# Edge pass of a graph attention layer: the group's transpositions on PE moved ahead of the encoding, their readers moved forward on DVE and ACT, the factor one step later

## The reference

```
h = (x @ W.T).reshape(n, H, D)                       # 6250 nodes, 8 heads of 32
alpha = sum(h[src] * a_src) + sum(h[dst] * a_dst)    # 200000 edges, sorted by dst
enc = relu(edge_attr @ edge_W.T + edge_b)
alpha = leaky(alpha + sum(enc * h[dst]))             # slope 0.2
amax = segment_max(alpha, dst)
ex = exp(alpha - amax[dst])
denom = segment_sum(ex, dst)
out = segment_sum(h[src] * ex / denom[dst], dst)
```

## Time and profile before

| | us |
| --- | --- |
| median of 3 runs | 5372.19 |
| lowest, highest | 5364.89, 5379.21 |
| profiled execution, own time | 5386.62 |
| its span, first to last instruction | 5384.8 |
| PE, DVE, ACT, POOL busy | 3894.4, 2587.7, 2125.3, 2060.0 |

### The profile page before, as it was taken

One profiled execution on the slowest core, in us unless ns is written; L12 is line 12 of the kernel. 1 busy time (PEld: TensorE's weight loads), 2 busy tenths in 40 slices (PEclk: granted clock), 3 DMA queues, 4 the chain that ended last, 5 costly groups with the idle time before them and its releaser, 6 DMA issues.

```text
span 5384.8 us, 88907 instructions
## 1 busy us (share of the span) xinstructions
PE 3894.4 (72%) x22054; PEld 2499.9 (46%) x22055; DVE 2587.7 (48%) x6056; ACT 2125.3 (39%) x5703; POOL 2060.0 (38%) x2172
## 2 busy tenths in 40 slices
PE   4778995676776666777676676666667767791999
PEld 3357884343343333333333333333333334580888
DVE  6556553554554455555454554454455546341121
ACT  3212331444444444444444444444444445342322
POOL 4120003454554454454444444444445443005111
PEclk8889998787787788788887887888788878895999
DMA  4610112333333333333333333333333332201110
GB/s 153 213 37 22 35 33 70 83 93 90 92 95 90 91 100 90 92 96 95 93 93 93 91 93 92 97 92 93 95 92 102 96 93 72 103 27 53 34 35 30
DMA packets 352302, 449.27 MB, mean 83 GB/s; under 512 B 170970, under 2 KB 275163, under 8 KB 350456
## 3 DMA queue, kind: packets, MB, share of 16 engines
q0 software_dynamic: 95568, 267.78, 19.0%
q10 hardware_dynamic: 108050, 122.83, 7.4%
q1 hardware_dynamic: 148231, 53.53, 4.1%
HBM read 389.57 MB, written 55.13 MB: 83 GB/s over the span
## 4 chain that ended last, share of the span: by engine, by line
PE 38%; another core or an unknown queue 21%; issue 11%; DVE 9%; ACT 9%; ACTq 7%; DMA 3%; DVEq 2%; POOL 1%; SPq 0%; POOLq 0%
ACT dist L770 5%; PE bank L1040 5%; PE bank L1183 4%; PE bank L1195 4%; PE bank L1061 3%; PE bank L1143 3%; PE bank L1005 3%; PE bank L1014 3%; ACTq L737 3%; PE bank L1099 3%; PE bank L1030 2%; ACTq L735 2%; DVEq L355 2%; DVE msg L1540 1%
## 5 line engine op out<-in xcount | busy, mean ns | idle before, releaser
L514 POOL DMA_INDIRECT al<-h_tab,idx x976 | 1022.8, 1048 | 1110.0 <-issue 1104.5
L752 ACT ACTIVATE enc<-bank,eb 128x512 f32<-128x512 f32 x880 | 556.3, 683 | 1768.5 <-remote 1213.1
L514 POOL DMA_INDIRECT gbuf<-h_tab,idx x784 | 793.4, 1012 | 906.4 <-issue 877.4
L1061 PE MATMUL bank<-prod,hsel 128*32 128x128 f32 x7040 | 351.1, 328 | 1001.4 <-DVE carry L1505 444.8
L1040 PE MATMUL bank<-oneh_t,hbt 125*128 125x512 bf16 x2640 | 865.1, 478 | 6.9 <-issue 3.5
L1061 PEld LDWEIGHTS bank<-prod,hsel 128*32 128x32 f32 x7040 | 200.3, 126 | 1190.2 <-DVE carry L1505 474.9
L1099 PE MATMUL bank<-msg,oneh 128*125 128x264 f32 x2352 | 648.2, 422 | 64.9 <-DVE r L1549 47.2
L1460 DVE SCALAR_TENSOR_TENSOR prod<-enc,adst,bank 128x512 f32<-128x512 f32 x880 | 629.4, 737 | 21.4 <-PE bank L1040 7.1
L770 ACT ACTIVATE dist<-iota_n,dtile 128x125 f32<-128x125 f32 x1760 | 550.8, 384 | 0.5
L1099 PEld LDWEIGHTS bank<-msg,oneh 128*125 128x125 f32 x2352 | 468.0, 207 | 173.1 <-issue 87.2
L1549 DVE TENSOR_TENSOR r<-r,bank 125x264 f32 x440 | 188.1, 428 | 614.7 <-issue 282.4
(11 more groups left out here) (255 smaller groups left out, 5747.7 us busy)
## 6 DMA issues: line engine op xcount, KB each, us to landing
dstb<-dst ACTq DMA_DIRECT2D x440, 125.0 KB
al<-pen_d SPq DMA_DIRECT2D x1760, 4.0 KB
att<-attrx ACTq DMA_DIRECT2D x880, 24.0 KB
al<-h_tab,idx POOLq DMA_INDIRECT x976
link<-links SPq DMA_DIRECT2D x880, 0.2 KB
gbuf<-h_tab,idx POOLq DMA_INDIRECT x784
attrx<-al ACTq DMA_DIRECT2D x8, 1176.0 KB, 12.3
hsplit<-hb POOLq DMA_DIRECT2D x25, 375.0 KB, 6.0
```

The lines of the kernel that those rows point to most:

```text
L514: pool.indirect_dma_start(slot(n)[:, c, :], None, h_tab, bass.IndirectOffsetOnAxis(ap=idx[g % 2][:, k:k + 1], axis=0)).then_inc(gathered[n ...
L752: m = act.activation(enc[n % 2][:, k, :], bank[k][:, :], ACT.Relu, bias=eb[:, k:k + 1])
L1061: m = pe.matmul(bank[7][32 * c:32 * c + 32, 0:128], hsel[:, i, :], prod[n % 2][:, k, c * 128:(c + 1) * 128], start=(i == 0 and k == 0), st ...
```

## The change

On PE `g_up` (lag 7), `g_down` (k%4==0) and `g_turn` (lag 10) move from behind `e_dst` to right behind `e_sum`, ahead of `e_enc`. The matmul of the delta leaves `g_up` for `g_down`, one step later. On DVE the ends with their chain, and the carry with its scans, move ahead of the one-hot and the message. On ACT `g_x` and `g_keep` move from the end of the step to right behind the relu, and `g_fac` goes from the end of step k%4==3 to the end of step k%4==0; it now waits for `ends_down` and `carry_read`. PE asks for the factor in step k%4==1, with the carry.

```diff
@@ ACT @@
             def g_fac(g):
-                act.wait_ge(ends_up, g + 2)
-                act.wait_ge(ends_read, min(g + 2, NG))
+                act.wait_ge(ends_down, g + 2)
+                act.wait_ge(carry_read, min(g + 2, NG))
...
                 if k < ITEMS:
                     e_relu(k)
+                if (g := group_at(k, 5)) is not None:
+                    g_x(g)
                 if (g := group_at(k, 9)) is not None:
                     g_exp(g)
+                if (g := group_at(k, 10)) is not None:
+                    g_keep(g)
...
-                if (g := group_at(k, 5)) is not None:
-                    g_x(g)
-                if (g := group_at(k, 10)) is not None:
-                    g_keep(g)
-                if (g := group_at(k, 11)) is not None:
+                if (g := group_at(k, 12)) is not None:
                     g_fac(g)
@@ PE @@
                 if k % G == 0:
                     wait(pe, ends_read, min((k - 8) // G, NG - 1) + 1)
-                    wait(pe, fac_ready, min((k - 8) // G, NG))
                 if k % G == 1:
                     wait(pe, carry_read, min((k - 9) // G, NG - 1) + 1)
+                    wait(pe, fac_ready, min((k - 9) // G, NG))
...
+                if (g := group_at(k, 7)) is not None:
+                    g_up(g)
+                if k % G == 0 and 8 <= k <= G * NG + 8:
+                    g_down((k - 8) // G)
+                if (g := group_at(k, 10)) is not None:
+                    g_turn(g)
                 if k < ITEMS:
                     e_enc(k)
                     e_dst(k, t[k % EB])
-                if k % G == 3 and 7 <= k <= G * NG + 7:
-                    g_up((k - 7) // G)
-                if (g := group_at(k, 8)) is not None:
-                    g_down(g)
-                if (g := group_at(k, 10)) is not None:
-                    g_turn(g)
@@ DVE @@
-                wait(v, ends_up, g + 1 if g else 0)
+                wait(v, ends_down, g + 1 if g else 0)
...
-                if k + 1 < ITEMS:
-                    e_onehot(k + 1, t_hot[k % G])
-                if 0 <= k - LM < ITEMS:
-                    m_msg(k - LM)
                 if g2 is not None:
                     g_ends(g2)
...
                     g_smax2(g3, known)
+                if k + 1 < ITEMS:
+                    e_onehot(k + 1, t_hot[k % G])
+                if 0 <= k - LM < ITEMS:
+                    m_msg(k - LM)
```

More of the change, by code:

```diff
@@ L1071, in g_up, with g_down @@
             def g_up(g):
[L1073 to L1076, removed]
+                pe.wait_ge(x_local, g + 1)
+                pe.matmul(bank[7][0:33, A0:A0 + 128], ends[0], ident[:, :], start=False, stop=False, skip_group_check=True)
+                pe.matmul(bank[7][0:33, A0:A0 + 128], ends[1], ident[:, ::-1], start=False, stop=False, skip_group_check=True).then_inc(ends_up, 1)
+            def g_down(g):
                 if g > 0:
@@ L1080, in g_up @@
                     m = pe.matmul(bank[7][0:P, B2:B2 + H], oneh[(G * (g - 1)) % NM][0:1, 0, :], dl[0:1, 1, :], start=False, stop=False, skip_group_check=True)
[L1081 to L1086, removed]
+                if g < NG:
+                    pe.wait_ge(links_made, g + 1)
+                    m = pe.matmul(bank[7][:, B0:B0 + 2], fin[:, :], ident[0:33, 0:33:32], start=False, stop=False, skip_group_check=True)
+                m.then_inc(ends_down, 1)
             def g_turn(g):
```

## The result

The changed kernel takes 5174.17 us (median of 3 runs, 5160.12 to 5196.96) against 5372.19: a ratio of 0.963, 95% interval 0.960 to 0.965. That is 198 us less, where 81 were forecast; the time lies inside the stated range, close to its fast end of 5150. The profiled execution took 5160.12 us.

What follows compares the result with a forecast made beforehand. Bound: POOL's gather batches and pauses in the edge pass, with PE's signals held late. 5386.62 - 102 + 21 = 5306, less 14.4 from profiled execution to median: 5291 us; range 5150 to 5500.

Steps and rivals of the forecast that it cites:

- The clock of the pass: Edge pass runs by POOL's gathers: PE's signals arrive late, 1.3 to 1.9 us behind a batch (the gate).
- Step (3): ACT, turned exponentials (L790) right behind the relu: PE comes about 1.9 us earlier; worth nothing by itself.
- rival C: PE matmuls before the carry really at work: 302 us less, 5070; its like: L1473 no longer stops; together chance 0.12.
- Step (1): DVE step k%4==0, carry and scans ahead of message: POOL's pause loses 1.46 us in 70 groups, 102 us less.
- step (4): ACT's factor moved to the end of step k%4==0, ready later: 0.3 us a group, 21 us more.
- B: Message behind a late carry: third gather batch, 5.3 us more pause; half the groups caught, 134 us more, 5506; chance 0.26.
- Step (2): DVE step k%4==3, ends, chain and sums ahead of message: the wait for L1080 (133.5 us) goes; costed at nothing.

Runs made afterwards that it cites:

- b_p3_turn: Kernel before, masked, with the turn alone (g_turn early on PE, g_x and g_keep early on ACT), no gate present: 4053.72 us, ratio 0.9788.
- d_p3_turn: The same turn-alone kernel run again, with the gate present: 5197.99 us beside 5381.0 of before, ratio 0.9672.
- b_g2_paced: Changed kernel, masked, plus a POOL wait: an item's gathers are issued only once those of the item before have landed; 5146.83 us, ratio 0.9573.

## Why the prediction was off

- **The clock of the pass** was read rightly. Without indirect gathers the pass runs at the speed of the runs without a gate, holding POOL back brings the start of the pass forward, and 140 of DVE's 155 long unnamed stops end within 1.0 to 2.2 us behind a batch. That was the mechanism, and it holds in the state that the prediction's trace shows; the prediction could not know that there is another.
- **Step (3) is the term that failed.** It was "worth nothing by itself" and, run by itself with the gate, measured 176 us. It counted PE's wait for L790 and called PE's idle time free. It left out what stands in the same diff hunk: `g_turn`, for which DVE's L1473 waits, 4.3 us a group. What the runs showed in its place: the pause behind L1473's step fell from 6.47 to 4.54 us a group. That stop had been seen in one group, at the end of the short batch, but was priced in no step; it was named only as a like of rival C, at a chance of 0.12. By the prediction's own rule, that only a shorter pause of POOL is worth time, the second pause (some 6 us) should have been gone through as the first was. How much of the whole change's 198 us hangs on this step stays open, since that pause is not shorter there.
- **Step (1)**, 102 us less, was never measured by itself with the gate. On top of the turn, the carry, the ends and the later factor give 0.9629 / 0.9672, about 24 us, give or take 20; with step (4) they were to give 81. But in the whole change the pauses around the carry are 1.5 us a group shorter, 165 us in 110 groups, more than the 102 forecast for them. They are not shorter in the forecast way: L1505 still stops 62 times where it stopped 70, for 4.2 us and not 6.8, and the batch is cut instead. So the size of (1) is open, and the account below for B says what is seen.
- **Step (2)**, nothing, is open with the gate. Without it, it gave 0.7 to 0.8% alone, and nothing is seen of it on top of the turn.
- **Step (4)**, 21 us: the waits stand where it put them, at L1532, 2.8 us each (299 us in 107 stops) and more than the 1.3 forecast. In the group shown the stop did not delay the next batch: DVE stopped for the factor at 3032.66 - 2.14 = 3030.52, with the message made, and POOL began on that message at 3031.30, 0.78 us later. The next message was late by it, which left 1.13 us of pause ahead of the third batch; over the pass there are 72 such pauses ahead of item 2, of 1.66 us. What the later place costs was not measured, with the gate or without.
- **Rival B** came true in its picture and not in its price. Batches of eight and four with L1505 waiting are there, in about half of the groups (54 pauses ahead of item 1), but the third batch starts after 1.13 us: 5.38, 1.13 and 6.46 make 12.97 us of pauses, against 7.55 + 6.02 = 13.57 before. 5.3 us more were forecast. The prediction's own argument against B held, that the message of the next step may follow the third without much of a pause. It also took the third batch for new; before had a pause ahead of item 1 in 36 of 106 groups.
- **Rival C**: the Trainium skill (Perfetto Trace Analysis, Summary: the profiler window per engine type) calls the end of a TensorE instruction an estimate; no trace here shows that end itself. The matmuls are the same in b_p3_turn and d_p3_turn, and of the 1144 us between them PE's busy time makes up 361, by the first part of both pages:

```profile
PE 3488.5 (86%) x22054; PEld 2378.5 (59%) x22055; DVE 2583.3 (64%) x6056; ACT 2115.6 (52%) x5703; POOL 2074.5 (51%) x2172
PE 3849.2 (74%) x22054; PEld 2524.6 (49%) x22055; DVE 2590.6 (50%) x6056; ACT 2107.6 (41%) x5703; POOL 2051.6 (39%) x2172
```

  Work of PE hidden behind the estimate would be there in both, but b_p3_turn has no unnamed stop in the pass. So it is not what the pass waits for, and C fell. Its like, that L1473 no longer stops, seems to have come in part: 4.3 us a group before, 159.0 / 110 = 1.4 after by DVE's row here. But in the whole change the stop has only moved to L1549, the instruction ahead of it (258 us of unnamed waits there before, 534 after, 900 to 4400 us), and the pause is as long as it was. With the turn alone it came as the rival has it, a stop gone, at 176 us and not 302.

```profile
L1473 DVE SCALAR_TENSOR_TENSOR al<-al 128x128 f32<-128x128 f32 x110 | 31.7, 288 | 159.0 <-remote 123.1 <-PE bank L1092 22.9 <-issue 13.0
```

## What to carry to other kernels

Once a clock has been found for a loop (here the pauses of one engine), go through every pause of a period, and list for each the signals that end it; price each instruction that the diff moves against that list, not against its own engine's idle time. An idle engine is not free if the signal behind its work has to be through before something else closes the door. Count such pauses over the whole loop and not in one period: a stop that is gone from one instruction may stand at its neighbour, with the pause unchanged. Parts measured alone need not add up when they act on the same clock. And a wait that keeps batches of indirect gathers short can pay for itself: b_g2_paced beats both kernels, at 5146.83 us, by an earlier start of the pass and not by shorter groups.

## What the runs showed of the hardware

- The same kernel took 5372 to 5381 us in some sets of runs and 4139 to 4147 in others, all of its 3 to 13 runs in a set alike. It is not the chip: one gave 5373 and later 4145, another 4139 and later 5381. With the short time no wait on an unnamed releaser is left, gathers run on almost without a pause (with the turn early, 0.31 us between two), and the granted clock is 0.957 against 0.84. So indirect gathers alone do not make the gate. What else it takes was not found; each kernel is compared only with the before that ran beside it.
- Direct DMAs of the same size on the same queue, from rows in a row, showed no late signals: 4151.9 us where before took 5373, in one run.
- Pauses of 2.6 to 2.8 us between batches of four gathers are enough for the carry's signal to come through (17 us of waiting in 110 groups), though DVE's L1475 still stops 99 times, for 401.5 us.
- With the gate, DVE's unnamed stops of over 4 us end mostly just behind the last gather of a batch, by a median of 1.5 us in before, 1.6 in after and 1.3 in b_g2_paced. With the turn alone 115 of 145 do (within 1.0 to 2.2 us), and 19 end while a batch runs.
